# Score pass of a four-layer graph network: masks from 8-bit signs, and three of four tiles of a product as three rounded products

## What is computed

```python
hW = h @ W
hp = (node_adj > 0).astype(hW.dtype) @ hW
hm = (node_adj < 0).astype(hW.dtype) @ hW
e_plus = jax.nn.leaky_relu(jnp.concatenate([hp, hm], axis=1) @ a, ALPHA)[:, 0]
e_minus = jax.nn.leaky_relu(jnp.concatenate([hm, hp], axis=1) @ a, ALPHA)[:, 0]
...
node_support = node_adj_norm @ h
edge_output = _gru_cell(node_support, h, edge_Wih, edge_Whh, edge_bih, edge_bhh)
```

## Time and profile before

| | |
|---|---|
| median of 3 runs | 2177.65 us (2176.7 to 2178.26) |
| the profiled execution, its own time | 2176.56 us |
| its span | 2174.6 us |
| TensorE busy | 1916.5 us, 88% of the span |
| VectorE busy | 1650.9 us, 76% |
| ScalarE busy | 1245.5 us, 57% |
| transfers | 489 MB, mean 225 GB/s |
| mean granted TensorE clock | 0.973 of full speed |

### The profile page before, as it was taken

How to read it: one execution, slowest core, us unless ns; L and a number is a source line. 1 busy time by engine, 2 the same in 40 slices (tenths; PEclk the granted TensorE clock), 3 DMA queues, 4 the chain that set the end, 5 groups by cost and what they waited for, 6 DMA issues and landing times.

```text
span 2174.6 us, 21337 instructions
## 1 busy us (share of the span) xinstructions
PE 1916.5 (88%) x7805; PEld 1166.7 (54%) x7805; DVE 1650.9 (76%) x2422; ACT 1245.5 (57%) x1386; POOL 0.8 (0%) x7
## 2 busy tenths in 40 slices
PE   2336999699979889879999959999999999999997
PEld 1224888478859888834444426644444444444443
DVE  4668998698849989855655743398898898888985
ACT  3445666366649898800000010198888788887873
POOL 0000000000000000000000000000000000000000
PEclk9999999899989999989999979999999999999998
DMA  9998999488857766659899749732333323233220
GB/s 389 429 429 349 344 338 345 166 306 319 321 194 252 247 222 249 232 181 334 298 321 324 272 162 326 248 99 109 107 122 106 111 102 126 95 118 126 91 83 10
DMA packets 81559, 489.46 MB, mean 225 GB/s; under 512 B 8449, under 2 KB 12546, under 8 KB 36402
## 3 DMA queue, kind: packets, MB, share of 16 engines
q1 hardware_dynamic: 77138, 485.94, 60.9%
q10 hardware_dynamic: 4320, 2.20, 0.3%
HBM read 452.36 MB, written 35.75 MB: 224 GB/s over the span
## 4 chain that ended last, share of the span: by engine, by line
PE 52%; DVE 11%; ACT 6%; issue 1%; DMA 0%; DVEq 0%
PE bank L1538 25%; PE bank L1426 11%; PE bank L1500 5%; PE bank L1394 4%; DVE work L1208 3%; ACT work L555 2%; ACT work L548 2%; PE bank L1421 2%; ACT work L551 1%; DVE reg L1208 1%; PE bank L1449 1%; PE bank L1450 1%; DVE ring L948 1%; PE bank L1520 1%; DVE work L1186 1%
## 5 line engine op out<-in xcount | busy, mean ns | idle before, releaser
L1538 PE MATMUL bank<-work,reg 128*128 128x512 f32 x960 | 423.1, 596 | 17.3 <-DVE ring L1157 11.4
L1208 DVE TENSOR_TENSOR work<-work,ring 128x1536 f32<-128x1536 f32 x160 | 280.5, 1753 | 67.7 <-ACT work L677 66.8
L853 DVE TENSOR_TENSOR a_lo<-ring,a_hi 128x2048 fp32r<-128x2048 f32 x128 | 290.8, 2288 | 31.4 <-ACT a_hi L502 30.5
L1538 PEld LDWEIGHTS bank<-work,reg 128*128 128x128 f32 x960 | 181.9, 191 | 246.7 <-issue 220.3
L502 ACT ACTIVATE a_hi<-ring 128x2048 fp32r<-128x2048 f32 x128 | 244.2, 1913 | 78.5 <-PE bank L1366 78.5
L1394 PE MATMUL bank<-reg,ring 128*128 128x129 f32 x2048 | 243.8, 281 | 34.3 <-DVE ring L948 34.3
L1394 PEld LDWEIGHTS bank<-reg,ring 128*128 128x128 f32 x2048 | 238.2, 197 | 39.2 <-DVE ring L948 29.3
L1538 PE MATMUL bank<-reg 128*128 128x512 f32 x576 | 252.4, 592 | 0.0
L677 ACT ACTIVATE work<-work 128x1536 f32<-128x1536 f32 x160 | 235.3, 1471 | 26.2 <-DVE work L1186 26.2
L1426 PE MATMUL bank<-ring,reg 128*128 128x512 f32 x512 | 237.8, 607 | 0.0
L1364 PE MATMUL bank<-a_hi,s_hi 128*128 128x512 f32 x512 | 207.4, 405 | 20.5 <-DVE a_lo L853 20.5
(11 more groups left out here) (215 smaller groups left out, 2158.1 us busy)
## 6 DMA issues: line engine op xcount, KB each, us to landing
ring<-in_adj_units SPq DMA_DIRECT2D x320, 1024.0 KB, 4.9
ring<-in_adj_rows SPq DMA_DIRECT2D x32, 2048.0 KB, 17.0
masks<-work SPq DMA_DIRECT2D x64, 512.0 KB, 8.9
ring<-masks SPq DMA_DIRECT2D x64, 512.0 KB, 4.6
reg<-lines SPq DMA_DIRECT2D x8, 768.0 KB, 10.2
ring<-lines SPq DMA_DIRECT2D x8, 768.0 KB, 7.9
out<-ring ACTq DMA_DIRECT2D x8, 256.0 KB, 2.3
gru<-in_cells SPq DMA_DIRECT2D x1, 768.0 KB
```

The source lines that it names most:

```text
L853: dve.tensor_tensor(a_lo[:, ring_at(p, g)], ring[:, ring_at(p, g)], a_hi[:, (g % 4) * UNIT:(g % 4 + 1) * UNIT].bitcast(F32), ALU.subtract) ...
L1208: dve.tensor_tensor(tv, tv, spread(ring[:, ring_at("out", g, q * W, W)], HEADS, 1), ALU.mult).then_inc(s_y, 1)
L1538: last = pe.matmul(bank[1 + k][:, :], h, tiles(c * T + t)[:, k * W:(k + 1) * W], start=t == 0, stop=t == T - 1)
```

## The change

- The masks: ScalarE takes the sign of the unit (2048 fp32) into an 8-bit buffer, two deep (`signs`, in `hn` and `hT`). The fp8 codes of 1 and -1 differ in the sign bit, so VectorE makes the masks by 32-bit logic on 512 words, four codes at a time: negative = (code >> 2) & 0x20202020, then positive = (code & 0x20202020) ^ negative. A set mask is now 0.125 and not 1, and the coefficients and two later sums are multiplied by 8.
- The product: the first tile of a unit stays fp32 (`WHOLE = 1`). For the other three ScalarE rounds 1536 columns into `edge_hi` (two units deep, in `a_hi`), VectorE subtracts it in place, and TensorE makes three rounded products of each. The node features are split the same way into `h_hi` and `h_lo`, once, during chunk 0.
- The order: ScalarE's program does `sign_of(n)` and `high_parts(n)` for every unit, with `keep_edge`, `gates` and `candidate` between them at g = 1, 4 and 5. `sign_of` waits for the unit's load, in the unit with g = c for its cleared diagonal, and for the masks of unit n - 2; `high_parts` waits for the product of unit n - 2. VectorE's masks wait for `s_sign`, its subtraction for `s_ehi`; TensorE waits for all of it. `cell_end`, `result` and `turn_cells` come one unit later, and the store of the masks goes by a semaphore of its own (`s_made`).

The core of the diff:

```diff
-        sums_sb = work[:, 4096:4096 + W]
+        sums_sb = outT[:, :]
+        signs = [b[:, 0:UNIT // 4] for b in (hn, hT)]
+        SPLIT = (Q - WHOLE) * W
+        def edge_hi(n):
+            return a_hi[:, 4096 + (n % 2) * SPLIT:4096 + (n % 2 + 1) * SPLIT]
...
             def store_masks(n):
-                sp.wait_ge(s_mask, n + 1)
+                sp.wait_ge(s_made, n + 1)
...
-            for c in range(1, C):
-                keep_edge(c)
-                gates("edge", c)
-                candidate("edge", c)
+            def sign_of(n):
+                c, g = n // G, n % G
+                act.wait_ge(*loaded("edge", c, g))
+                if c == g:
+                    act.wait_ge(s_fix["edge"], g + 1)
+                if n > 1:
+                    act.wait_ge(s_made, n - 1)
+                act.activation(signs[n % 2].bitcast(FP8), ring[:, ring_at("edge", g, c=c)],
+                               ACT.Sign, saturate=False).then_inc(s_sign, 1)
+            def high_parts(n):
+                c, g = n // G, n % G
+                if n == 0:
+                    act.wait_ge(s_mm["gat"], G * C)
+                    act.wait_ge(s_pkeep["gat"], C * U_STEPS)
+                if c == 0:
+                    act.wait_ge(s_hkept, g + 1)
+                    act.activation(h_hi[:, g * W:(g + 1) * W], reg1[:, g * W:(g + 1) * W],
+                                   ACT.Copy).then_inc(s_hhi, 1)
+                if n > 1:
+                    act.wait_ge(s_mm["edge"], n - 1)
+                act.activation(edge_hi(n), ring[:, ring_at("edge", g, WHOLE * W, SPLIT, c=c)],
+                               ACT.Copy).then_inc(s_ehi, 1)
+            for c in range(C):
+                for g in range(G):
+                    if c and g == 1:
+                        keep_edge(c)
+                    if c and g == 4:
+                        gates("edge", c)
+                    if c and g == 5:
+                        candidate("edge", c)
+                    sign_of(c * G + g)
+                    high_parts(c * G + g)
...
             def masks(n):
                 c, g, b = n // G, n % G, n % MASKS
-                dve.wait_ge(*loaded("edge", c, g))
                 if c == g:
+                    dve.wait_ge(*loaded("edge", c, g))
                     clear_diagonal("edge", g)
...
-                src = ring[:, ring_at("edge", g, c=c)]
-                dve.tensor_scalar(made[b][0], src, 0.0, None, ALU.is_gt, saturate=False)
-                dve.tensor_scalar(made[b][1], src, 0.0, None, ALU.is_lt, saturate=False).then_inc(s_mask, 1)
+                dve.wait_ge(s_sign, n + 1)
+                code = signs[n % 2].bitcast(I32)
+                plus, minus = (m.bitcast(I32) for m in made[b][0:2])
+                dve.tensor_scalar(minus, code, 2, NONZERO, ALU.logical_shift_right,
+                                  ALU.bitwise_and).then_inc(s_neg, 1)
+                dve.wait_ge(s_neg, n + 1)
+                dve.scalar_tensor_tensor(plus, code, NONZERO, minus, ALU.bitwise_and,
+                                         ALU.bitwise_xor).then_inc(s_made, 1)
+                if c == 0:
+                    dve.wait_ge(s_hhi, g + 1)
+                    dve.tensor_tensor(h_lo[:, g * W:(g + 1) * W], reg1[:, g * W:(g + 1) * W],
+                                      h_hi[:, g * W:(g + 1) * W].bitcast(F32), ALU.subtract).then_inc(s_hlo, 1)
+                dve.wait_ge(s_ehi, n + 1)
+                rest = ring_at("edge", g, WHOLE * W, SPLIT, c=c)
+                dve.tensor_tensor(a_lo[:, rest], ring[:, rest], edge_hi(n).bitcast(F32),
+                                  ALU.subtract).then_inc(s_mask, 1)
...
-                    if c and g == 3:
+                    if c and g == 4:
                         cell_end("edge", c, s)
-                    if c and g == 5:
+                    if c and g == 6:
                         result("edge", c)
...
-                    last = pe.matmul(nacc[:, :], reg1[:, t * P:(t + 1) * P],
-                                     ring[:, ring_at("edge", g, q * W, W, c=c)], start=t == 0, stop=t == T - 1)
+                    part, tile = ring_at("edge", g, q * W, W, c=c), slice(t * P, (t + 1) * P)
+                    if q < WHOLE:
+                        pe.matmul(nacc[:, :], reg1[:, tile], ring[:, part], start=t == 0, stop=False)
+                        continue
+                    hi = edge_hi(n)[:, (q - WHOLE) * W:(q - WHOLE + 1) * W]
+                    pe.matmul(nacc[:, :], h_hi[:, tile], hi, start=t == 0, stop=False)
+                    pe.matmul(nacc[:, :], h_hi[:, tile], a_lo[:, part], start=False, stop=False)
+                    last = pe.matmul(nacc[:, :], h_lo[:, tile], hi, start=False, stop=t == T - 1)
...
-                    if c and g == 4:
+                    if c and g == 5:
                         turn_cells("edge", c)
```

More of the change, by code:

```diff
@@ L24 @@
 EPS = 1e-5
+NONZERO = 0x20202020
+MASK_VALUE = 0.125
 SLOPE = 0.2
@@ L33 @@
 EPAD = 32
+WHOLE = 1
 SCORES = 2 * HEADS
@@ L112, in build @@
         reg2 = sb("reg2", [P, N])
+        h_hi = shared("h_hi", [P, N], F32R)
         reg3 = sb("reg3", [P, N + T])
+        h_lo = shared("h_lo", [P, N], F32R)
         reg4 = sb("reg4", [P, N + W])
@@ L268, in build @@
         s_mask = sem("edge_masks")
+        s_sign, s_neg, s_made = sem("edge_signs"), sem("edge_negative_masks"), sem("edge_masks_made")
+        s_hhi, s_hlo, s_ehi = sem("edge_h_high"), sem("edge_h_low"), sem("edge_unit_high")
         s_stored = [sem(f"masks_stored{b}") for b in range(MASKS)]
@@ L869, in _ @@
             dve.memset(spv[:, :, ECOLS - 1:EPAD], 0.0)
-            dve.memset(smv[:, :, ECOLS - 1:ECOLS], 1.0)
+            dve.memset(smv[:, :, ECOLS - 1:ECOLS], 1 / MASK_VALUE)
             dve.memset(smv[:, :, ECOLS:EPAD], 0.0)
@@ L907, in gat_project @@
                 dve.wait_ge(s_proj["gat"], c)
-                s.link(dve.tensor_copy(u, bank[4][:, 0:HS]))
+                s.link(dve.tensor_scalar(u, bank[4][:, 0:HS], 1 / MASK_VALUE, None, ALU.mult))
                 s.link(dve.tensor_copy(spc[:, :, 0:SCORES], uv))
@@ L1107, in norm_nodes_in @@
                 dv = dsum.rearrange("p (t v) -> p t v", v=KW)
-                s.link(dve.tensor_copy(dv, vv[:, :, 2 * KW:3 * KW]))
-                s.link(dve.tensor_tensor(dv, dv, vv[:, :, KW:2 * KW], ALU.add))
-                s.link(dve.tensor_tensor(dv, dv, vv[:, :, 0:KW], ALU.add))
+                s.link(dve.tensor_scalar(dv, vv[:, :, 2 * KW:3 * KW], 1 / MASK_VALUE, None, ALU.mult))
+                for part in (1, 0):
+                    s.link(dve.scalar_tensor_tensor(dv, vv[:, :, part * KW:(part + 1) * KW], 1 / MASK_VALUE, dv,
+                                                    ALU.mult, ALU.add))
                 s.link(dve.tensor_scalar(dok, dsum, WINDOW_MIN, None, ALU.is_ge))
```

## The result

The changed kernel takes **2182.72 us** (20 runs, 2179.74 to 2185.1), beside 2178.2 for the kernel before on the same chip: ratio 1.002, 95% interval 1.0014 to 1.0027. It is 4.5 us slower. The prediction had called up to 4.4 us "within 0.2%"; the interval, 3.0 to 5.9 us, lies on both sides of that bound. The profiled execution took 2184.61 with a span of 2182.8, so it is 1.9 above the median; its span is 8.2 longer than that of the kernel before.

What follows compares the result with a forecast made beforehand. TensorE was taken to bound the score pass. Chunks 1 to 7 at -0.3 us, chunk 0 at -0.7 and transfers at +1.5 gave +0.5 on 2177.65, so 2178, range 2165 to 2197.

Steps and rivals of the forecast that it cites:

- The unit: TensorE's work for one unit of the score pass: 4.18 us falls by 0.51 to about 3.66.
- The operations: ScalarE and VectorE per unit: sign 1.91 us, rounding 1.47, rest 1.75, shift 0.43 (or 0.69), xor 0.69.
- Unit 1: Chunks after chunk 0: TensorE stalls 1.85 us because keeping sums and support precedes the unit's sign, rounding and rest.
- Unit 6: Chunks after chunk 0: TensorE stalls 0.80 us because the cell's end stands before this unit's masks on VectorE.
- The cleared diagonals: Unit c of chunks 4 to 7: the sign waits for VectorE's clearing; together +10.1 us.
- The start: Chunk 0: clearing, sign, roundings and rest in a row start TensorE at 948.25 instead of 945.04, +3.2 us.
- Transfers: Score pass: enough cover in the later chunks, +1 to +2 us in chunk 0, DMA share near 0.95.
- The clock: Fourth rival, score pass: the granted clock falls in TensorE's new gaps; chance 0.02, inside the slower cases.
- TensorE stays the bound: Faster rival, score pass: engines run further ahead and stalls fall away, 2147.5 us; chance 0.25.
- Transfers decide: Slower rival, score pass: stores land later than 11.5 us, units run at 4.31 us, 2203 in all; chance 0.10.
- Another table set: Slower rival, ScalarE: sign needs another table set than tanh, four switches a chunk, 36 us, 2214 in all; chance 0.03.
- The estimate of 41 us: TensorE's saving in the score pass if a rounded product takes a quarter of an fp32 tile, 0.214 us.

Runs made afterwards that it cites:

- e3: Changed kernel, with ScalarE making the sign of unit 1 before it keeps the sums of the chunk before; 2170.13 us, ratio 0.9962.
- e6: Changed kernel with one more load of 128 KB, not used, in every unit of the score pass; 2183.86 us, ratio 1.0025.
- e5: Changed kernel with unused TensorE products in its gaps: six before unit 1 of chunks 1 to 7, eight before unit c of chunks 4 to 7; 2174.94 us.
- e10: e9 with three unused fp32 products on TensorE between the last projection and the score pass; 2156.0 us, ratio 0.9896.
- e11: e10 with the result of the chunk before placed between the masks of units 1 and 2; 2144.51 us, ratio 0.9844.
- e7: Changed kernel with the moves of e3 and e4 together; 2154.28 us, ratio 0.9887.
- e4: Changed kernel, with VectorE clearing a diagonal block two units ahead; 2168.82 us, ratio 0.9962.
- e8: e7 with the first diagonal cleared before the last projection of the pass ahead; 2151.41 us, ratio 0.9877.
- e9: e8 with the cell's end spread behind units 5, 6 and 7, cells turned after unit 7, result after the next chunk's unit 2; 2157.72 us.
- after: The changed kernel itself, without any follow-up edit; 2182.72 us, ratio 1.002 to the kernel before.

## Why the prediction held, point by point

The prediction was 2178, "same" likeliest, with 2165 to 2197 as its range. Measured: 2182.7, and 4.5 us against its bound of 4.4. The mechanism of the sum was right: TensorE's shorter unit is given back in waits at the places that were named. One step of it failed, the clock. Its steps:

- **The unit.** 3.66 was forecast. Where nothing stands between two units, their starts are 3.66 to 3.70 apart in every chunk, and the change-over from fp32 to rounded products, which the trace of before didn't show, cost at most the 0.03 left over.
- **The operations.** Sign 1.90 (1.91), rounding 1.48 (1.47), rest 1.76 (1.75), shift 0.43 (0.43, so the long end of 0.69 fell), xor 0.69 (0.69).
- **Unit 1.** Forecast 1.85; measured 6.21 - 3.69 - 0.80 = 1.72 in each chunk. e3 took it away by changing the order of two calls.
- **Unit 6.** Forecast 0.80; measured 4.54 - 3.69 - 0.41 = 0.44. Half of it was too much.
- **The cleared diagonals.** Forecast 2.4, 2.2, 3.2 and 2.3 in chunks 4 to 7 and none before; measured 2.05, 2.03, 3.23, 2.29 and none. The clearing of 1207.21 in chunk 6, the sign, the rounding, the rest and TensorE's unit 6, one behind the other:

```profile
1207.21 0.89 DVE L1006 TENSOR_TENSOR ring<-ring,offdiag 128x128 f32<-128x128 f32 x4
...
1208.19 1.91 ACT L612 ACTIVATE hn<-ring 128x2048 fp8e4<-128x2048 f32 x1 [4.74 <-issue]
...
1210.01 1.47 ACT L627 ACTIVATE a_hi<-ring 128x1536 fp32r<-128x1536 f32 x1
...
1211.51 1.76 DVE L1035 TENSOR_TENSOR a_lo<-ring,a_hi 128x1536 fp32r<-128x1536 f32 x1
...
1213.32 1.05 PE L1481 MATMUL bank<-work 128*32 128x512 fp8e4 x8 [3.57 <-DVE a_lo L1035]
```

- **The start.** Forecast 3.2 later; measured from the end of the clearing 5.83 instead of 2.54, 3.3 later.
- **Transfers.** Forecast +1.5, and a share of 0.95. Both were too much: 0.81 over the chunks, no wait for stored masks, 8.2 us to land one:

```profile
masks<-work SPq DMA_DIRECT2D x64, 512.0 KB, 8.2
```

By e6 there was cover for 8% more bytes.
- **The clock** is the step that failed. I gave its fall 0.02 and took a stretch with a clock of 1.00 as evidence, for "gaps like these". Looked at one by one, the three waits of TensorE in it, all for VectorE's rest, are of 1.11, 1.13 and 1.11 us, shorter than the 1.65 us and more of the score pass. Whether the length is what matters wasn't tried. The balance of chunks 1 to 7 in the profiled execution: -27.4 from the shorter unit (56 x 0.49), +12.0 at unit 1, +3.1 at unit 6, +9.6 at the cleared diagonals; that is -2.7, where I had -0.3 (and -0.5 if 7 x 1.51 is carried out, 10.6 and not 10.4). Measured is +7.4. The rest of 10.1 is six lengthened places: 1.6 in each of chunks 2, 6 and 7 between units 1 and 2, 1.2 in chunks 4 and 5, 2.9 in chunk 6. All lie behind a gap. In e5 all are gone but 0.25 in each of chunks 4 and 5, which follow from the late unit there and not from the clock. In chunk 0, unit 0 took 6.49 where the 5.61 of before, less 0.5, gives 5.1: +1.4, also the clock, as e10 shows. That place varies from trace to trace: e6, with the same idle time ahead of it, has 5.24.

So 2182.7 came of three errors: chunks 1 to 7 taken 2.4 us too long, the transfers 1.5 too dear, and the clock left out, worth 7.8 by e5 and 1.4 more in unit 0. Together they give 2183.5. Beside e5, which has the gaps and not the falls in chunks 1 to 7, my forecast is 3 us too high. The range held, but its upper part had been meant for longer hand-overs and a dear change-over, not for this; and two of the errors hid part of the third. That much of the agreement is luck.

Of the rivals, "TensorE stays the bound" gave 2147.5 for a kernel without stalls. e11 has one stall left in chunks 1 to 7 (0.87 us, in chunk 3) and stands at 2144.5. Its pass starts 2.8 us earlier than the rival's. Other differences of 1 to 2 us each (unit 0 at the full clock, a unit that saves 0.49 and not 0.52, a wait of 1.8 in chunk 0, the 2 us behind the pass) partly cancel, so the two agree to a few us. The rival's sum was about right, and what kept the changed kernel from it was the order of the work and the clock, not the amount of it. "Transfers decide" fell with e6, and with e7 also for chunks of 36.3 us. "Another table set" fell: the one load in the pass (L596) is that of tanh, which stood there before. The Trainium skill, in ScalarE: Activation LUTs, section on precision budgets, lists sign with relu and identity. That list is of accuracy and says nothing of loads; that sign needs none of its own is what this trace shows.

The estimate of 41 us from the Trainium skill's count of passes (FP8 and Floating Point Precision, TensorE Precision Notes) didn't come true: 64 x 0.49 is 31. The measurement decides; most of the shortfall is a start every 0.23 us rather than 0.214 for a rounded product.

## What to carry to other kernels

When work moves from the engine that bounds a pass to two that were idle, their averages say little: with buffers two deep, each step that another engine's result must pass through stands in the row, and a few places a chunk decide. Follow one chunk by its waits, and put what nobody waits for (keeping a sum, clearing a block, a cell's end) behind what somebody does; here four such moves (e3, e4, e8, and e9 with e11's correction), with three unused products ahead of the pass, turned +4.5 us into -34. Before moving a step later, look for who reads or overwrites its bank: e9 lost 6 us that way.

## What the hardware showed that I had not expected

A gap of 1.65 us in a TensorE that was busy otherwise was followed by stretches with a granted clock of 0.77, 0.50 and 0.88, and cost 1.6 us beside itself. The same gap at unit 1 did this in some chunks and not in others, and not in the same ones in every trace: in e6 it was chunks 1, 2 and 7, in after 2, 6 and 7. It may be why the runs of after lie 5.4 us apart and those of before 2.9. The mean clock of the four slowest runs of after is 0.967, that of the four fastest 0.969 to 0.970, and the runs of e5 lie 3.0 apart; a second trace of after, which would show it, wasn't taken. Products whose results nobody reads, put into the gaps, took 7.8 us off the kernel. Whether fewer than six and eight would do wasn't tried.
